# New order of preparation and fill, and two of five PSUM copies on ScalarE, in a patch-attention kernel

## The reference

```python
n = gn(x)
embed = prelu(conv1x1(n, Wa, ba)); match = prelu(conv1x1(n, W1, b1))
ref = prelu(conv1x1(mean_pool_2x2(n), W2, b2))
raw_w = patches(embed, 6, stride 2)            # 576 keys
w = patches(ref, 3, 1); wn = w / max(norm(w), 1e-4)
yi = softmax(10 * einsum(wn, patches(match, 3, 1)), over the 576 keys)
yt = transposed_conv(yi, raw_w, stride 2)
yd = conv3x3(yt, Wd, stride 2) + bd
x1 = x + yd / 6
out = x1 + DCT_h DCT_w gn(x1)                   # cosine transform over rows and columns
```

## Time and profile before

| what | value |
| --- | --- |
| median of 3 runs | 242.66 us (242.5 to 242.75) |
| the profiled execution's own time | 243.28 us |
| its span, first to last instruction | 241.5 us |
| busy: TensorE / VectorE / ScalarE / GpSimd | 187.8 / 169.2 / 104.4 / 114.0 us |
| mean granted clock of TensorE | 0.873 of 2.4 GHz |
| preparation: to the first maximum | 37.39 us |
| fill: to the scores of tile 10 | 76.08 us |

### The profile page before, as it was taken

The page is one execution under the profiler, slowest core; times in us unless marked ns, Lnnn a source line. Parts: engine busy times, 40 slices in busy tenths (PEclk is TensorE's granted clock), DMA queues, the critical chain, the costliest instruction groups (busy, mean ns, idle before and its releaser), DMA issues.

```text
span 241.5 us, 3419 instructions
## 1 busy us (share of the span) xinstructions
PE 187.8 (78%) x1140; PEld 154.0 (64%) x1140; DVE 169.2 (70%) x343; ACT 104.4 (43%) x185; POOL 114.0 (47%) x109
## 2 busy tenths in 40 slices
PE   0498264875759997699999799989988899991484
PEld 0456164764548986588778688777666588870482
DVE  4776736594454878789896888888989664777502
ACT  4564324486475447554647664546243110000110
POOL 3075600195155872445997346575549974000000
PEclk9999557789575799989999999999999999998555
DMA  7960496158003500912131000003113000002502
GB/s 162 218 117 14 75 119 119 57 110 197 0 0 54 80 0 7 131 24 77 48 100 50 0 4 0 1 3 75 22 48 94 5 0 3 0 0 50 100 0 49
DMA packets 11409, 13.37 MB, mean 55 GB/s; under 512 B 7760, under 2 KB 8320, under 8 KB 10960
## 3 DMA queue, kind: packets, MB, share of 16 engines
q1 hardware_dynamic: 10992, 12.64, 27.0%
q10 hardware_dynamic: 400, 0.52, 0.8%
HBM read 4.41 MB, written 1.18 MB: 23 GB/s over the span
## 4 chain that ended last, share of the span: by engine, by line
PE 50%; DVE 24%; ACT 9%; issue 8%; DMA 4%; SPq 2%; ACTq 1%; POOL 0%; DVEq 0%; POOLq 0%
PE zt L806 14%; PE yt L822 13%; PE ps L785 10%; DVE negm L1216 5%; ACT nt L975 4%; PE pm L842 3%; DVE bnst L1038 3%; DVE v L1246 3%; DVE ys L1231 3%; DMA par<-params 2%; DVE mimg L1125 2%; DMA v<-mimg 2%; ACT slanted L930 2%; PE pm L832 2%; SPq L414 1%
## 5 line engine op out<-in xcount | busy, mean ns | idle before, releaser
L594 POOL TENSOR_TENSOR nt<-nt 128x599 f32<-128x599 f32 (+1 forms) x54 | 73.7, 1365 | 49.6 <-ACT nt L983 39.9
L806 PEld LDWEIGHTS zt<-ident,nt 128*125 128x125 f32 (+1 forms) x420 | 54.6, 181 | 15.2 <-issue 2.7
L806 PE MATMUL zt<-ident,nt 128*125 128x128 f32 (+1 forms) x420 | 57.7, 279 | 0.9 <-POOL nt L594 0.9
L822 PE MATMUL yt<-ys,ek 125*128 125x384 f32 (+1 forms) x120 | 50.7, 504 | 5.6 <-DVE ys L1231 5.5
L983 ACT ACTIVATE nt<-nt,rps 128x599 f32<-128x599 f32 x36 | 28.7, 796 | 30.2 <-DVE rps L1223 30.1
L1231 DVE COPY ys<-zt 125x384 f32<-125x384 f32 (+1 forms) x60 | 32.6, 553 | 10.2 <-PE zt L806 6.5
L975 ACT ACTIVATE nt<-ps,negm 128x576 f32<-128x576 f32 x32 | 23.7, 739 | 36.2 <-DVE negm L1216 36.2
L785 PE MATMUL ps<-wh,mh 128*128 128x288 f32 x64 | 19.6, 392 | 14.3 <-DVE mr L1211 6.9
L1216 DVE TENSOR_REDUCE negm<-ps 128x1 f32<-128x576 f32 x32 | 24.1, 752 | 7.5 <-PE ps L785 6.9
L1246 DVE SCALAR_TENSOR_TENSOR v<-yt,v 32x384 f32<-32x384 f32 (+3 forms) x48 | 26.3, 547 | 2.5 <-PE yt L822 1.0
L822 PEld LDWEIGHTS yt<-ys,ek 125*128 125x128 f32 (+1 forms) x120 | 18.6, 192 | 9.2 <-DVE ys L1231 9.0
(11 more groups left out here) (150 smaller groups left out, 270.9 us busy)
## 6 DMA issues: line engine op xcount, KB each, us to landing
nt<-nt SPq DMA_DIRECT2D x12, 285.2 KB, 3.0
xuv<-x SPq DMA_DIRECT2D x8, 281.9 KB, 5.9
vim<-mimg SPq DMA_DIRECT2D x8, 144.0 KB, 4.2
v<-x SPq DMA_DIRECT2D x2, 288.0 KB, 10.2
vim<-mimg SPq DMA_DIRECT2D x8, 72.0 KB, 2.6
x_copy<-v SPq DMA_DIRECT2D x2, 288.0 KB, 2.7
xr<-x_copy SPq DMA_DIRECT2D x4, 144.0 KB, 3.1
out<-res SPq DMA_DIRECT2D x8, 72.0 KB, 2.3
```

The costliest lines, as they stand in the source:

```text
L594: pool.tensor_tensor(nt[:, dst, (to + 1) * KP + 1:(to + 1) * KP + 1 + n], nt[:, one, (row1 + 1) * KP + 1:(row1 + 1) * KP + 1 + n], nt[:, o ...
L806: last = nc.tensor.matmul(turned_thirds(zt[:, m % 2, :], n, col), keys_at(tile, r + dr, n, shift), ident[:, :], start=at == 0, stop=at == ...
L822: nc.tensor.matmul(yt[:, k % 2, 0:CHUNK], ek[b][0:n, blk, :], ys[0:n, blk, :], start=blk == 0, stop=blk == KB - 1).then_inc(s_mb, 1)
```

## The change

BEFORE has a new order: bias_1 ahead of conv2, all conv1 parts in a row, norm and inorm behind them, mean of image 1 behind those, and only chunk 0's split. SPREAD moves most of image 1's jobs later and farther apart; the split of chunk 1 goes into the fill. GpSimd waits for the first scores before it clears the shifted tiles. One of three ninth-tap DMAs of chunk 0 is issued from SyncE's queue between groups 0 and 1. COPIES gives blocks 1 and 3 of each chunk to ScalarE, where they stand in front of the step's exp; VectorE keeps blocks 0, 2 and 4, in their places. The semaphore of copies is split in two, one for each engine.

```diff
 BEFORE = [
-    ("xs", 0, (0,)), ("mean", 0, (0,)), ("weights", 0, (0,)), ("bias_2", 0, (0,)), ("xs", 1, (0,)), ("conv2", 0, (0, 1)),
-    ("squares", 0, (0,)), ("bias_1", 0, (0,)), ("conv1", 0, (0, 1)), ("mean", 1, (0,)), ("conv1", 0, (2, 3, 4, 5)),
-    ("norm", 0, (0,)), ("conv1", 0, (6, 7)), ("inorm", 0, (0, 1)),
-    ("ninth", 0, (0,)), ("keys", 0, (0, 1)), ("split", 0, (0, 1))]
+    ("xs", 0, (0,)), ("mean", 0, (0,)), ("weights", 0, (0,)), ("bias_2", 0, (0,)), ("bias_1", 0, (0,)), ("xs", 1, (0,)),
+    ("conv2", 0, (0, 1)), ("squares", 0, (0,)), ("conv1", 0, (0, 1, 2, 3, 4, 5, 6, 7)), ("norm", 0, (0,)), ("inorm", 0, (0, 1)),
+    ("mean", 1, (0,)), ("ninth", 0, (0,)), ("keys", 0, (0, 1)), ("split", 0, (0,))]
 SPREAD = [
-    ("weights", 1, 1, 0, 1), ("bias_2", 1, 1, 1, 1), ("conv2", 1, 2, 2, 1), ("wst", 0, 1, 2, 1), ("bias_1", 1, 1, 4, 1),
-    ("bias_a", 0, 1, 5, 1), ("squares", 1, 1, 6, 1), ("emb", 0, 2, 7, 2), ("conv1", 1, 8, 11, 1.5), ("ek", 0, 2, 14, 2),
-    ("norm", 1, 1, 25, 1), ("inorm", 1, 2, 30, 2), ("wst", 1, 1, 31, 1), ("keys", 1, 2, 34, 3), ("bias_a", 1, 1, 34, 1),
-    ("residual", 0, 1, 36, 1), ("emb", 1, 2, 39, 2), ("ek", 1, 2, 45, 2), ("residual", 1, 1, 60, 1),
+    ("weights", 1, 1, 0, 1), ("bias_2", 1, 1, 1, 1), ("wst", 0, 1, 2, 1), ("conv2", 1, 2, 2, 2), ("bias_1", 1, 1, 5, 1),
+    ("bias_a", 0, 1, 6, 1), ("squares", 1, 1, 7, 1), ("emb", 0, 2, 8, 2), ("conv1", 1, 8, 12, 2.2), ("ek", 0, 2, 16, 4),
+    ("norm", 1, 1, 29, 1), ("inorm", 1, 2, 34, 2), ("wst", 1, 1, 34, 1), ("keys", 1, 2, 38, 3), ("bias_a", 1, 1, 37, 1),
+    ("residual", 0, 1, 36, 1), ("emb", 1, 2, 40, 2), ("ek", 1, 2, 46, 2), ("residual", 1, 1, 60, 1),
...
+COPIES = ("dve", "act", "dve", "act", "dve")
...
-    starts += [(3 * TPC * g - SPLIT_LEAD, "split", g // NCH, g % NCH) for g in range(2, NG)]
+    starts += [(max(3 * TPC * g - SPLIT_LEAD, 1), "split", g // NCH, g % NCH) for g in range(1, NG)]
...
+        def wait_copied(eng, m):
+
+            who = COPIES[m % KB]
+            eng.wait_ge(s_ys[who], COPIES.count(who) * (m // KB) + COPIES[:m % KB + 1].count(who))
...
+                    if b == 0 and t == 0:
+                        at = 1 + 2 * CHUNK + SHIFTS[2][0]
+                        sp.dma_start(v2[0:CR, 0:CHUNK], mimg[64:64 + CR, at:at + CHUNK]).then_inc(s_nin[0], 16)
...
             perform(before, handlers)
+            pool.wait_ge(s_sc, 1)
             shifted_tiles(DOWN0, 1)
...
-                    pe.wait_ge(s_ys, m - 1)
+                    wait_copied(pe, m - 2)
...
-                pe.wait_ge(s_ys, KB * k + blk + 1)
+                wait_copied(pe, KB * k + blk)
...
-                for n in range(3):
+                for n in (1, 2):
                     nc.scalar.dma_start(v2[CR * n:CR * (n + 1), 0:CHUNK],
...
+            def sums_copied(k, blk):
+
+                n, m = KEYS[blk], KB * k + blk
+                act.wait_ge(s_zt, m + 1)
+                if k:
+                    act.wait_ge(s_mb, m - KB + 1)
+                nc.scalar.activation(ys[0:n, blk, :].rearrange("p (h j) -> p h j", j=W), turned(zt[:, m % 2, :], n),
+                                     ACT.Copy).then_inc(s_ys["act"], 1)
...
                 if s < FILL:
                     softmax(s)
+                if k >= 0 and j == 1:
+                    sums_copied(k, 1)
+                if k >= 0 and j == 2:
+                    sums_copied(k, 3)
                 if s + 1 < NT:
                     exp(s + 1)
...
-                if k >= 0 and j == 1:
-                    sums_copied(k, 1)
-                if k >= 0 and j == 2:
-                    sums_copied(k, 3)
                 if s + 1 == FILL:
                     inverse_sum(s)
```

More of the change, by code:

```diff
@@ L291, in program @@
         s_zt = sem("sums_turned")
-        s_ys = sem("sums_copied")
+        s_ys = {"dve": sem("sums_copied_dve"), "act": sem("sums_copied_act")}
         s_mb = sem("taps_block_done")
@@ L1013, in _ @@
             for s in range(steps):
+                k, j = s // TPC - LAG, s % TPC
                 if s < FILL:
                     softmax(s)
+                if k >= 0 and j == 1:
+                    sums_copied(k, 1)
+                if k >= 0 and j == 2:
+                    sums_copied(k, 3)
                 if s + 1 < NT:
@@ L1231, in sums_copied @@
                 nc.vector.tensor_copy(ys[0:n, blk, :].rearrange("p (h j) -> p h j", j=W),
-                                      turned(zt[:, m % 2, :], n)).then_inc(s_ys, 1)
+                                      turned(zt[:, m % 2, :], n)).then_inc(s_ys["dve"], 1)
             def finish(k, n):
```

## The result

The changed kernel takes 237.8 us as the median of 4 runs (235.5 to 241.12), against 242.59 for the kernel before beside it (242.5 to 242.75, 4 runs). The ratio is 0.9715, with a 95% interval of 0.9691 to 0.9738. The forecast was 238.4 us, a range of 234.0 to 244.2, and a chance of 0.75 for faster: direction, time and range hold.

What follows compares the result with a forecast made beforehand. TensorE was taken as the bound in 108-166 and 192-218 us, wait chains in preparation and fill. Terms -0.4, -1.0 and -3.3 sum to -4.7, rounded to 4.3 for overlap: 238.4 us, range 234.0 to 244.2.

Steps and rivals of the forecast that it cites:

- Preparation: before the first scores and first maximum: -0.4 us, between +1.5 and -1.6.
- (c): preparation: first image copy no longer under GpSimd's memset, 0.96 us go; match image ready some 1.9 us earlier.
- (d): preparation: norm behind conv1 parts and image copies, so inverse root runs from 23.75 instead of 21.40; scaled keys end near 29.2.
- (b): preparation: eight conv1 parts without mean, norm and bias between them; last PReLU ends about 1.0 us earlier.
- Fill with what it hands on: fill to 76 and the work handed to chunk 0: -1.0 us, between +2.5 and -5.0.
- I let the first idle shrink by 1.5 us, and the second by 0.6: fill: TensorE's 2.91 us idle, conv1 waiting for a PReLU, and 2.69, scores waiting for exp(8), both shrink.
- Copies: 24 of 60 copies moved from VectorE to ScalarE: -3.3 us, between 0.5 slower and 5.0 faster.
- no change of note: rival: removed stalls return under other names, such as the reciprocal; 241.7 us, chance 0.14.
- the zero of the plain chunks: undisturbed chunks: ScalarE's copy fits into its 1.95 us idle before exp, so worth nothing and costs nothing.
- Slower: rival: late norm's serial chain, second split before maximum(2), handed work paid in chunk 0; 245.0 us, chance 0.19.
- More: rival: fill opens, both its idles go (5.0 us), and copies give 3.3; 234.0 us, chance 0.14.
- a new stretch at half clock behind the fill: behind the fill: listed among the signs that would show the forecast wrong; no size given.

Runs made afterwards that it cites:

- after: the changed kernel itself, in its one profiled execution of 241.12 us; median of its runs 237.8 us.
- e3: changed kernel with chunk 1's split back in the preparation, in front of the first maximum: 239.75 us, ratio 0.9862.
- e10: kernel before with one line more, GpSimd's wait for the first scores before its memsets: 240.41 us, ratio 0.9898.
- e5: changed kernel without GpSimd's wait for the first scores before its memsets: 240.24 us, ratio 0.9769.
- e6: changed kernel with image 0's norm ahead of the last two conv1 parts and mean 1 behind the split: 238.16 us, ratio 0.9742.
- e4: changed kernel with the SPREAD of the kernel before: 241.03 us, ratio 0.9824.
- r_after: changed kernel, unchanged, run and profiled again on another chip: 237.26 us, ratio 0.9728.
- e1: kernel before with only the copies of blocks 1 and 3 on ScalarE, in front of exp: 239.87 us, ratio 0.9895.
- e2: changed kernel with all five copies back on VectorE in their old places: 239.79 us, ratio 0.9875.
- e9: changed kernel with ScalarE's copies behind the step's exp instead of in front of it: 244.39 us, ratio 1.0067.
- e7: changed kernel with the column pair of chunk 9 moved from GpSimd to VectorE: 241.86 us, ratio 0.9951.
- e8: changed kernel with both the early norm of image 0 and chunk 9's column pair on VectorE: 239.48 us, ratio 0.9866.

## Why the prediction was right, and where it was not

**Preparation (forecast -0.4).** Near in size at each milestone: first scores 0.4 to 1.9 us later (forecast 1.5), first maximum 1.5 to 2.3 earlier (1.6), third maximum 0.6 to 1.0 earlier (0.4). The first copy at 0.33 us, the late root and the two steps (c) and (d) are as written; (b) is open, since the copy starts 12.7 us behind the weights in after and 14.1 and 12.9 in the two profiles before. The attribution behind the first maximum failed. The moved split holds 0.4 to 0.6 us there (e3). The memset's wait, which I had let the late norm eat, holds 1.3 to 1.4 wherever the norm stands (e10, e5), and the late norm and mean take 2.5 back (e6). These don't add up to the gain, so the parts depend on each other, or what is left of the new order (the eight conv1 in a row, bias_1, the moved DMA) holds 2 to 3 us that no run isolates. That the memset and the weights cost nothing beside the fill fits the timeline, where the split falls beside the second memset with its usual lengths.

**Fill with what it hands on (forecast -1.0).** The direction is right, the size too small (2.0 to 2.8 us by e4), and the way there is not the forecast one. The step that failed is "I let the first idle shrink by 1.5 us, and the second by 0.6". The conv1's wait for a PReLU, 2.91 and 2.95 us in the two profiles before, is 2.68 in after and 2.67 or 2.68 in all other profiles with the new SPREAD but r_after. (There it is 0.54, as the scores in front of it ran at half clock; the conv1 starts at the same moment, 59.83 against 59.92.) Together with the wait for exp(8) it makes 5.6 and 5.4 us before and 4.9 in after: 0.5 to 0.8 less, and not 2.1. What changed is where that wait stands: before, and in e4, it is in front of the scores of tile 7, now behind them. From maximum 6 to 7 it takes 3.4 us in after, against 6.8 before and 6.9 in e4, and that is nearly all that the fill gains up to maximum 10, 3.5 to 4.2 us. What it handed on (conv1, copies, norm) cost there more than my 1.1, some 3.3, but part of it came back by maximum 17, where the old order pays too.

**Copies (forecast -3.3).** The sum is right, 2.7 to 3.5 us; its division is not. Chunk 1 was to give 2.0; from maximum 11 to 17 it is 28.8 us in e1 against 30.2 and 30.4 before, and 26.3 and 26.4 in the changed kernel against 27.4 in e2, so 1.0 to 1.6. The wait for the copy went, but exp stood behind it with 1.23 us, and the half clock that I charged with 0.8 isn't there in every execution and is worth little: the kernel before takes 30.4 us with it and 30.2 without. Chunks 7 and 8 were to give 1.3. Behind maximum 35 three waits of 1.87 together became one of 1.76: that is the mechanism of the rival "no change of note", a removed stall that comes back under another name. The 0.9 us that came there all the same (56.7 to 55.8) are the last copy's 0.32, forecast as nothing, 0.1 of the waits named, and some 0.5 that no single wait shows. The waits of chunks with a split stayed, as forecast, and e9 shows what cover the zero of the plain chunks rests on.

**The rivals.** "Slower" was to decide at maximum(2) behind 43.1 and a fill ending behind 76.5. Maximum(2) started at 41.16 by the clock of the trace (33.9 to 32.9 from the weights), so it had fallen at its first point. "More" gave 234.0 with both idles gone; in after one of 2.68 and one of 1.36 for a conv1 stay, and one of 2.17 and one of 0.85 for exp, and still the two shortest runs, 235.5 and 235.9, lie between it and the forecast.

**The sum.** The measured terms are -0.6 to -1.0, -2.0 to -2.8 and -2.7 to -3.5: -5.3 to -7.3 together, against my -4.7 and the -6.9 of the ratio. I rounded down to 4.3 for overlap, and none shows: the terms lie in different stages. That the median of 237.8 sits near my 238.4 is in part luck. Two of its four runs took 239.7 and 241.1 us; the second is the profiled one and carries the 4.8 us stretch, which no term of mine had, and the terms were too small by about half of that. I had named "a new stretch at half clock behind the fill" as what would speak against me, and it came.

**Open.** What starts the stretch. The wait of 1.75 to 1.77 us for GpSimd in front of it stands in e1, e3, e5 and e6 as well, whose profiled executions keep 2.4 GHz there. e7 and e8, where it is 1.30 and 1.31, have the stretch. Open too is what the clock does in the fill from one execution to the next; in e6 and e8, one program up to there, maximum 11 is 1.2 us apart with it, and each experiment has one profile.

## What to carry to other kernels

A copy given to a less busy engine is worth what its place in the queue makes of it: in front of an instruction that waits anyway no TensorE wait was put down to it here and it gained some 3 us, and moved behind that instruction it cost some 8. Keep GpSimd's clearing of buffers away from VectorE's single-input copies and casts on a serial chain, and look for the new victim when the order changes; one wait gave 1.4 us. When work is moved out of a fill, follow the milestones beyond the point where it is paid, since the gain at the fill's end (4 us) and the gain just behind it (under 1) both mislead about what stays (2 to 3). And profile one program twice before a milestone is trusted: here two executions of one differed by 2.1 us.

## What the runs showed of the hardware that I had not expected

- With the same wait in front of it, TensorE's granted clock falls to half for 10.3 us in some executions and not in others. That costs 4.8 us of 236.
- Beside a memset of 1.60 us a cast of 16x288 took 1.72 us instead of 0.30: it ended just behind the memset, as the image copy did before.
- Beside GpSimd's row sums a copy of 96x336 took 1.61 us instead of 0.33, and a subtraction of 16x384 with two inputs 1.76 instead of 0.66.
- With a sum and two normalisations on VectorE beside them, four GpSimd sums took 6.27 us against 5.85.
- Without any change to the program before it, a stretch of 9.8 us around the end of the fill was granted 0.52 of the clock in one execution and 0.84 in another.
- The arrival of the parameters moves the first scaling of weights by up to 1.3 us between executions, so milestones have to be counted from it.
